# The product of minus one, mean and inverse deviation: one VectorE reduction over three columns of a tile in place of a two-input operation

## The reference

```python
mod = (_silu(L0_c) @ L0_wmod).reshape(L0_c.shape[0], 6, 1, -1)
sa, ca, ga, sb, cb, gb = (mod[:, 0], mod[:, 1], ..., mod[:, 5])
ga = (2 * (ga >= 0) - 1) * jnp.maximum(jnp.abs(ga), 0.25)
gb = (2 * (gb >= 0) - 1) * jnp.maximum(jnp.abs(gb), 0.25)
h = _layernorm(x, axis=-1) * (1 + ca) + sa
x = x + ga * _L0_attn_ref(h, ...)
h = _layernorm(x, axis=-1) * (1 + cb) + sb
x = x + gb * _L0_ffn_ref(h, ...)
```

```python
dA = jnp.exp(A[None] * dtt[..., None])
dB = dtt[..., None] * bt[:, None, :]
h = dA * h + dB * xt[..., None]
y = jnp.sum(h * ct[:, None, :], axis=-1)
```

## Time and profile before

| | us |
|---|---|
| median of 3 runs | 4452.8 |
| lowest and highest of them | 4450.74, 4457.69 |
| the profiled execution's own time | 4458.12 |
| its span, first to last instruction | 4456.4 |
| granted TensorE clock, mean over the span | 0.969 of full speed |

### The profile page before, as it was taken

The page is one execution under the profiler, slowest core; times in us unless marked ns, Lnnn a source line. Parts: engine busy times, 40 slices in busy tenths (PEclk is TensorE's granted clock), DMA queues, the critical chain, the costliest instruction groups (busy, mean ns, idle before and its releaser), DMA issues. The chain is left out here.

```text
span 4456.4 us, 68965 instructions
## 1 busy us (share of the span) xinstructions
PE 4097.4 (92%) x21664; PEld 2562.2 (57%) x21664; DVE 3759.8 (84%) x5133; ACT 3825.2 (86%) x6371; POOL 3664.6 (82%) x2218
## 2 busy tenths in 40 slices
PE   7999999999999999999999999999999999999987
PEld 3655565655565555655555656555655555555554
DVE  3788888888888888888888888888888888888884
ACT  3888898888898888988888988888988889888884
POOL 2898888888888888888888888888888888888883
PEclk8899999999999999999999999999999999999998
DMA  4566665666665666666676656666656666656764
GB/s 148 115 140 152 142 147 123 143 145 150 147 147 121 144 149 146 146 132 129 142 157 141 145 124 138 145 149 147 139 124 148 150 147 145 135 129 141 158 135 85
DMA packets 260961, 622.84 MB, mean 140 GB/s; under 512 B 31068, under 2 KB 33116, under 8 KB 260600
## 3 DMA queue, kind: packets, MB, share of 16 engines
q0 software_dynamic: 117248, 369.14, 45.5%
q1 hardware_dynamic: 143352, 249.29, 17.3%
HBM read 281.70 MB, written 34.64 MB: 71 GB/s over the span
## 5 line engine op out<-in xcount | busy, mean ns | idle before, releaser
L411 POOL TENSOR_TENSOR work<-work,c_bc 128x1024 f32<-128x1024 f32 x1024 | 2618.5, 2591 | 455.8 <-DVE work L1218 268.0
L1218 DVE TENSOR_TENSOR_SCAN work<-work,state,b_ps 128x512 f32<-128x512 f32 x1792 | 2235.4, 1271 | 223.7 <-PE b_ps L526 212.5
L925 ACT ACTIVATE work<-u_td,b_td 128x512 f32<-128x512 f32 x2048 | 1453.6, 710 | 99.4 <-PE b_ps L526 90.5
L915 ACT ACTIVATE work<-dt_t,neg_a 128x512 f32<-128x512 f32 x2048 | 1451.7, 709 | 43.7 <-DVE work L1218 43.7
L526 PE MATMUL b_ps<-ident,work 128*128 128x128 f32 x8192 | 1231.2, 280 | 246.6 <-DVE work L1218 188.7
L526 PEld LDWEIGHTS b_ps<-ident,work 128*128 128x128 f32 x8192 | 979.9, 144 | 812.8 <-DVE work L1218 410.8
L601 PEld LDWEIGHTS y_ps<-ident,work 128*128 128x128 f32 x4096 | 475.6, 143 | 123.8 <-issue 122.8
L422 POOL DMA_DIRECT2D work<-work x512 | 492.5, 1013 | 60.6 <-POOL work L411 41.6
L601 PE MATMUL y_ps<-ident,work 128*128 128x128 f32 x4096 | 536.3, 276 | 0.7 <-DMA work<-work 0.7
L704 PE MATMUL dense<-h_t,w_in_t 128*128 128x512 f32 x1024 | 523.5, 638 | 1.0 <-ACT h_t L929 1.0
L675 PE MATMUL dense<-w_out_t,proj 128*128 128x512 f32 x1024 | 515.8, 606 | 0.0
(11 more groups left out here) (112 smaller groups left out, 4366.2 us busy)
## 6 DMA issues: line engine op xcount, KB each, us to landing
work<-work POOLq DMA_DIRECT2D x512, 512.0 KB, 5.6
c_bc<-c_d SPq DMA_DIRECT2D x512, 256.0 KB, 3.4
xn<-in_x SPq DMA_DIRECT2D x128, 256.0 KB, 7.0
work<-xs_t POOLq DMA_DIRECT2D x64, 512.0 KB, 7.7
x<-in_x SPq DMA_DIRECT2D x128, 256.0 KB, 5.2
x<-par_d POOLq DMA_DIRECT2D x64, 512.0 KB, 7.3
x<-par_d POOLq DMA_DIRECT2D x32, 1024.0 KB, 10.8
out_dram<-x SPq DMA_DIRECT2D x128, 256.0 KB, 4.1
```

The lines of the kernel that those rows point to most:

```text
L411: gp.tensor_tensor(made_here, both(hs, HS_RING, s * U + i), c_bc[:, (s * N + n) % C_RING:(s * N + n) % C_RING + 1, :].to_broadcast([P, 2, ...
L915: A(decay[:, (s * U + i) % DEC_RING, :], dt_t[:, s % 2, j, :], ACT.Exp, scale=neg_a[:, j, n:n + 1]).then_inc(S["dec_done"], 1)
L925: A(v[:, n % V_RING, tb, :], u_td[:, tb, :], ACT.Copy, scale=b_td[:, s % 2, tb, n:n + 1]).then_inc(S["v_done"], 1)
L1218: V.tensor_tensor_scan(hs[:, (s * U + i) % HS_RING, :], decay[:, (s * U + i) % DEC_RING, :], b_ps[:, i % 2, :], state[:, i:i + 1] if s % N ...
```

## The change

`minus_mean` was a `scalar_tensor_tensor` with two inputs in SBUF: column 6 times -1 times column 9. It becomes a `tensor_reduce` with a multiplication over one input in SBUF, 4 x 3 elements: columns 6, 9 and 12 (a step of three). Column 12 is new and holds -1, written once by a `memset` at VectorE's start. So `norm` is 13 columns wide instead of 10, and the tiles allocated behind it (`eps`, `c_bc`, `work`) begin 144 bytes later in each partition. A new semaphore `sign_set` orders the `memset` before the reduction; its wait stands behind the one that was there. The order of all other instructions on every engine is as before.

```diff
-        norm = sb("norm", [P, 3, TB, 10])
+        norm = sb("norm", [P, 3, TB, 13])
...
+            V.memset(norm[:, :, :, 12:13], -1.0).then_inc(S["sign_set"], 1)
...
             def minus_mean(n, k, rstd, nmr):
                 dve.wait_ge(S[rstd], at(rstd, k, 1))
-                V.scalar_tensor_tensor(norm[:, n, :, 8:9], norm[:, n, :, 6:7], -1.0, norm[:, n, :, 9:10], ALU.mult,
-                                       ALU.mult).then_inc(S[nmr], 1)
+                dve.wait_ge(S["sign_set"], 1)
+                V.tensor_reduce(norm[:, n, :, 8:9], norm[:, n, :, 6:13:3], mybir.AxisListType.X, ALU.mult
+                                ).then_inc(S[nmr], 1)
```

More of the change, by code:

```diff
@@ L200, in build_program @@
         w2dg_done b_out_loaded bout_done moved_ps moved c_exp c_one c_rcp silu_c rows_ps rows_taken mods_ps mods_done sign_done gate_done par_made
-        par_stored bout_row bout_made bout_added gs_loaded wg_loaded wout_done""".split()
+        par_stored bout_row bout_made bout_added gs_loaded wg_loaded wout_done sign_set""".split()
         PER = {
```

## The result

The changed kernel takes 4312.69 us (median of 4 runs, 4308.26 to 4317.61) against 4454.47 for the kernel before, measured again beside it: a ratio of 0.968, 95% interval 0.9665 to 0.9699. The profiled execution's span went from 4456.4 to 4315.2 us, which is 141.2 us less. One execution of all, 4959.94 us at a mean granted clock of 0.801, of the first run under "Filling ScalarE's wait", is left out of every comparison.

What follows compares the result with a forecast made beforehand. No engine is full (TensorE 92%); they wait for each other in turns, so a joint standstill costs most. 105 us of stall plus 47 of clock less 13 for GpSimd, rounded to 140, gave 4313 us, range 4278 to 4362.

Steps and rivals of the forecast that it cites:

- The stall: VectorE's n = 2 product behind slot 31 waits for GpSimd's product; the reduction would not: 118.9 us less on VectorE.
- How much of it is on the path: TensorE behind the n = 2 product: 0.45 us of catching up lost in each of 31 steps, leaving 105 of 118.9 us.
- The clock: TensorE's clock falls behind its idle 3.58 us; 26 low stretches at 1.8 us would come back, 47 us.
- B: Rival: stall comes back but the clock does not, or another wait takes up the rest; 4335 to 4360, chance 0.24.
- One of its signs: TensorE's busy sum would be lower by some 44 us, as low-clock matmuls count double.
- GpSimd's deduction: GpSimd's gaps offer 4.4 us where nearer 5.4 a step is needed; half of that 1 us charged for 26 steps, 13 us.
- rival C: GpSimd paces the step, only its idle 2.60 us returns; about 4372; sign: no gap for 20 us behind slot 31; chance 0.09.
- The new wait: Wait ahead of VectorE's reduction, fulfilled from the start: issue cost 0 to 0.06 us each, 64 times; taken as 0.
- The sum: Whole span: 139 us, rounded to 140, off the profiled 4458.1 gives 4318; median of runs forecast at 4313 us.
- F: Rival: 144 bytes by which c_bc and work move make DMA into and between them slower; kernel slower, chance 0.03.
- E: Rival: the reduction is held up like the operation before it and nothing changes; 4453, chance 0.03.
- D: Rival: low-clock stretches elsewhere go too, 15 at 1.8 us, 27 us more; 4260 to 4288, chance 0.09.

Runs made afterwards that it cites:

- Filling ScalarE's wait: Its first run: kernel before with ScalarE's four normalizing passes one slot later; 4461.3 us, ratio 1.0006. Second: same move in the changed kernel; 4315.12 us.
- six delays: Changed kernel with six bn_stats of 128x512 ahead of the n = 2 reduction in all steps but the last; 4447.05 us, ratio 0.9974.
- three delays: Changed kernel with three bn_stats of 128x512 ahead of the n = 2 reduction in all steps but the last; 4340.3 us, ratio 0.9738.
- the slot 32 run: Kernel before, two-input operation kept, with the n = 2 product moved behind slot 32's scan; 4405.48 us, ratio 0.988.
- the last one: Changed kernel with the four copies of y_ps behind slots 6, 6, 7, 7 instead of all behind slot 6; 4279.29 us, ratio 0.9601.
- the filler: Kernel before with six more repeats of slot 33's four transposes on TensorE; 4420.05 us, ratio 0.9914. Same in the changed kernel: 4394.28 us, 0.986.
- The run with the widened tile: Changed kernel with the two-input operation put back, keeping the 13 columns, memset, new wait and moved addresses; 4460.46 us, ratio 1.0009.
- the run with the late n = 0 product: Kernel before with the n = 0 product one slot later (nmrx=17); 4456.2 us in a single run, next to 4455.34.

## Why the prediction was right, and which terms were off

- **The stall.** It was right. A two-input operation waited for GpSimd's product, the reduction does not; 0.16 us each was foreseen and 0.17 measured, 118.9 us of VectorE's time and 118.3 measured. The same operation one slot away waits too, and `tensor_scalar` does not.
- **How much of it is on the path.** The step that took TensorE's 0.45 us of arrears off (31 x 0.45 = 14 us) stays open. Counted with half of the low-clock time, both artificial delays cost their full length within 6 us, which speaks against it. TensorE's own busy time, and its idle time as the rest of the span, speak for it. These are the engine lines of the runs with six and three delays, and with the old operation behind slot 32:

```profile
PE 4102.2 (92%) x21664; PEld 2562.8 (57%) x21664; DVE 3752.7 (84%) x5320; ACT 3823.9 (86%) x6371; POOL 3665.5 (82%) x2218
...
PE 4046.5 (93%) x21664; PEld 2535.1 (58%) x21664; DVE 3694.2 (85%) x5227; ACT 3820.9 (88%) x6371; POOL 3668.4 (84%) x2218
...
PE 4057.2 (92%) x21664; PEld 2540.5 (58%) x21664; DVE 3752.9 (85%) x5133; ACT 3828.1 (87%) x6371; POOL 3667.5 (83%) x2218
```

Against the changed kernel the idle time is 104.8 us more with six delays and 38.4 with three, for delays of 110.3 and 55.1. And the 141.2 us of the change itself are 101.2 us less idle and 40.0 us less busy time, where the forecast had 105 and 47. No run decides between the two reckonings.
- **The clock.** The price of a stretch was about right, the number was not. 1.8 us a stretch was foreseen; 102 us less low-clock time gave 52.5 us in the slot 32 run, which is 1.75 us for a stretch of 3.4, 92 us less gave 43.0 in the last one, 1.6, and 85 us less gave 48.7 with the filler, 1.95. But 26 stretches were counted back, 47 us, and the low-clock time fell by 58 us, which is 17 stretches or 29 us. Those behind slot 31 did all go; others, 108 to 112 us behind the n = 0 product, became longer. The forecast named such a move as a rival (B) and gave it all or nothing, and it happened in part. One of its signs came out near its number all the same: TensorE's busy time fell by 40.0 us, with 44 foreseen.
- **GpSimd's deduction.** The 13 us were charged since GpSimd would have no room. It did run without a gap there, from 1953.84 to 1996.27 in the trace of the changed kernel, and in 23 of 30 steps for more than 20 us behind the reduction (gaps under 0.1 us not counted). The sign named for rival C, such a stretch of 20 us, thus came true although C's time, 4360 to 4395, did not; it was a poor sign. Whether GpSimd's spare time later in the step took up all of the 13 us is not shown.
- **The new wait.** Its price of 0 to 0.06 us each was given without a row. The run with the widened tile has it 64 times and shows no cost (1.0009).
- **The sum.** 105 + 47 - 13 was forecast. By delay and half of the low-clock time the runs give about 118 + 29 less some 6: two deductions too many and a clock term too large that cancelled out. By TensorE's idle and busy time they give 101 + 40. In either reckoning single terms are off by 4 to 18 us, so a time of 4313 against 4312.69 is partly luck.
- **The rivals.** Slower by the moved tiles (F) is refuted by the run with the widened tile. No change (E) is refuted by the result. More than the forecast (D) was there to be had, 36 us, but by another edit. By the prediction's own chances its range leaves out more than the stated 0.16: C, E and F make 0.15, and the far half of D some 0.05.

## What to carry to other kernels

Where a tiny VectorE instruction has a mean ten times its median, put its long instances beside GpSimd's timeline: if each ends with GpSimd's work, remake it with one streamed SBUF input, as a reduction over columns or as `tensor_scalar`. When a stall goes, count the granted clock behind it as a gain of its own, but look for the next idle place of TensorE before counting it in full: part of the low clock moves there. Cutting such a place in two, by one scan between four copies, was worth a quarter of the whole change.

## What had not been expected of the hardware

A delay of 1.78 us a step cost 27.5 us of span over 31 steps, and one of 3.56 us cost 149.6 (25 and 130 us by the ratios): twice the delay, five times the price. The low-clock time went from 99 us to 48 in the one and to 167 in the other, and TensorE's busy time by -10.9 and +44.8 us. And 744 matmuls that compute nothing new made the kernel before 38 us faster, since they kept TensorE at 2.4 GHz through a stall in more of the steps.

A waiting VectorE operation is also not let in at the first end of a GpSimd operation: that of 2030.26 began to wait while the gate L490 ran, and ran itself only behind the product L411 that GpSimd began at 2031.50. The issue L422 lies between the two, and these are its rows:

```profile
2030.90 1.14 POOL L422 DMA_DIRECT2D work<-work  x1
2031.50 2.90 POOL L411 TENSOR_TENSOR work<-work,c_bc 128x1024 f32<-128x1024 f32 x1
```

GpSimd's records overlap from L490 to L411, so it has no gap before 2034.40. The traces of the six runs with the old operation have 216 instances of it longer than 0.2 us. Of these, 215 end 0.02 to 0.04 us after the first moment at which no record of GpSimd is open, and 154 of the 216 have a GpSimd product, gate or addition end before that without being let in. So on record the operation waits for the end of GpSimd's unbroken work. In the run with the late n = 0 product, 9 of the n = 2 instances even begin between gate and product, up to 0.28 us before the product, while L422 runs alone, and wait all the same. In four of them there would have been time for the 0.16 us. One of them, with GpSimd's rows:

```profile
2438.29 3.21 DVE L1231 SCALAR_TENSOR_TENSOR norm<-norm 128x4 f32<-128x4 f32 x1 [1.20 <-ACT norm L1006]
...
2436.75 1.51 POOL L490 TENSOR_TENSOR sz_t<-sz_t,tmp 128x512 f32<-128x512 f32 x1
2437.97 1.13 POOL L422 DMA_DIRECT2D work<-work  x1
2438.57 2.89 POOL L411 TENSOR_TENSOR work<-work,c_bc 128x1024 f32<-128x1024 f32 x1
```

An issue that stands alone does not hold it up: the short instance at 2130.35 runs inside L429. What in such a chain keeps it out stays open. In the changed kernel GpSimd's chain goes on for 29.2 us behind the reduction; behind the old operation it ends at 2034.40, with a gap of 2.60 us.
